# A causal mask of a chunked scan: one full mask product per group of heads against extra rows in the difference products plus 64x64 products on the diagonal

## The reference, cut to what matters

```
decay = exp(dt_t * a)
b_bar = dt_t[..., None] * b_t
state = decay * state + b_bar[..., None] * x_t[:, :, None, :]
y_t   = einsum('bhn,bhnp->bhp', c_t, state)
```

## Time and profile before

| | |
|---|---|
| median of 3 runs | 1465.38 us (1464.57 to 1468.33) |
| the profiled execution | 1465.41 us |
| its span, first to last instruction | 1463.4 us |
| TensorE matmuls, busy | 1403.8 us (8803 instructions) |
| TensorE weight loads, busy | 862.6 us |
| DVE / ACT / POOL, busy | 996.6 / 689.1 / 308.5 us |
| granted TensorE clock, mean | 0.988 of full speed |

### The profile page before, as it was taken

One profiled execution on the slowest core, in us unless ns is written; L12 is line 12 of the kernel. 1 busy time (PEld: TensorE's weight loads), 2 busy tenths in 40 slices (PEclk: granted clock), 3 DMA queues, 4 the chain that ended last, 5 costly groups with the idle time before them and its releaser, 6 DMA issues.

```text
span 1463.4 us, 23472 instructions
## 1 busy us (share of the span) xinstructions
PE 1403.8 (96%) x8803; PEld 862.6 (59%) x8803; DVE 996.6 (68%) x2849; ACT 689.1 (47%) x1351; POOL 308.5 (21%) x386
## 2 busy tenths in 40 slices
PE   8999999999999999999999999999999997999984
PEld 4447645676457665576456764576655763567543
DVE  2426797477874787477974778747874779747682
ACT  4443543645455562635436454555626354462312
POOL 3004201341104301142013411043011420133110
PEclk9999999999999999999999999999999998999998
DMA  8000001020000100020010200001000200101010
GB/s 299 10 0 30 15 15 48 3 75 29 26 23 17 61 30 26 22 78 15 15 48 2 76 30 26 22 18 61 29 26 22 77 15 15 47 4 46 29 48 4
DMA packets 47552, 54.24 MB, mean 37 GB/s; under 512 B 7625, under 2 KB 42313, under 8 KB 47441
## 3 DMA queue, kind: packets, MB, share of 16 engines
q1 hardware_dynamic: 41424, 46.41, 9.5%
q0 software_dynamic: 6016, 6.35, 1.7%
HBM read 34.84 MB, written 17.85 MB: 36 GB/s over the span
## 4 chain that ended last, share of the span: by engine, by line
PE 85%; DVE 8%; issue 4%; ACT 1%; POOL 1%; DMA 0%; POOLq 0%; SPq 0%; DVEq 0%
PE ps L1563 41%; PE ps L1729 8%; PE ps L1678 5%; PE ps L1637 4%; PE ps L1630 4%; DVE yst L1166 3%; PE ps L1690 2%; PE ps L1649 2%; PE ps L1869 2%; PE ps L1879 2%; PE ps L1664 2%; PE ps L1655 2%; PE ps L1668 1%; PE ps L1834 1%; PE ps L1800 1%
## 5 line engine op out<-in xcount | busy, mean ns | idle before, releaser
L1563 PE MATMUL ps<-xT,wb_s 128*128 128x512 f32 x512 | 232.9, 601 | 3.6 <-ACT xT L722 3.5
L1563 PE MATMUL ps<-xT,wc_s 128*128 128x512 f32 x512 | 225.4, 593 | 0.0
L1563 PEld LDWEIGHTS ps<-xT,wc_s 128*128 128x128 f32 x512 | 96.1, 190 | 112.3 <-issue 111.9
L1563 PEld LDWEIGHTS ps<-xT,wb_s 128*128 128x128 f32 x512 | 94.1, 191 | 113.1 <-issue 104.5
L1047 DVE SCALAR_TENSOR_TENSOR xT<-xc,cols_s,xT 128x512 f32<-128x512 f32 x192 | 134.8, 748 | 2.7
L1563 PE MATMUL ps<-hT,wx_s 128*128 128x512 f32 x256 | 117.7, 603 | 1.6 <-ACT hT L680 1.2
L1563 PE MATMUL ps<-hT,wz_s 128*128 128x512 f32 x256 | 112.8, 593 | 0.1
L1729 PE MATMUL ps<-CT,xT 128*128 128x256 f32 x512 | 111.9, 379 | 0.9 <-DVE xT L1226 0.9
L747 ACT ACTIVATE BT<-ps 128x512 f32<-128x512 f32 x64 | 37.9, 592 | 150.4 <-PE ps L1563 150.4
L1729 PEld LDWEIGHTS ps<-CT,xT 128*128 128x128 f32 x512 | 97.2, 190 | 17.8 <-issue 5.0
L788 ACT ACTIVATE XB<-ps 128x512 f32<-128x512 f32 x64 | 38.3, 599 | 138.0 <-PE ps L1649 138.0
(11 more groups left out here) (299 smaller groups left out, 2637.5 us busy)
## 6 DMA issues: line engine op xcount, KB each, us to landing
xr<-x SPq DMA_DIRECT2D x8, 1024.0 KB, 9.2
x_scratch<-xr SPq DMA_DIRECT2D x32, 256.0 KB, 2.1
out<-EC SPq DMA_DIRECT2D x32, 256.0 KB, 2.1
BT<-x SPq DMA_DIRECT2D x7, 1024.0 KB, 5.6
modrow<-mod_scratch SPq DMA_DIRECT2D x8, 512.0 KB, 6.6
w_s<-w SPq DMA_DIRECT2D x2, 1024.0 KB, 11.5
BT<-x SPq DMA_DIRECT2D x2, 512.0 KB, 5.2
xT<-wmod SPq DMA_DIRECT2D x1, 1024.0 KB, 9.4
```

Source lines behind the costliest of these rows:

```text
L1563: ins = t_.matmul(bank[:, :], w[:, k, m * P:(m + 1) * P], rhs[:, k, half * HALF:(half + 1) * HALF], start=k == 0, stop=k == nk - 1)
```

## The change

The full mask products are gone. The mask of a 128x128 block (source token j on the partitions, target token i along the columns) has four 64x64 blocks: j < 64, i >= 64 is never masked; j >= 64, i < 64 is masked as a whole; the two on the diagonal are the same triangle. The wholly masked block now comes out of the difference products by one more row per head: `Lsrc` has 1 in its columns 24 to 27 (of each half) for tokens 64 to 127, `Rsrc` has -1e30 there for tokens 0 to 63. These rows were zeros and were part of the products already. The two triangles are added by 64x64 products with the identity, one for each bank and each diagonal block, with 4 x 64 columns that stand 128 apart in the bank. The difference products now open the banks, and the wait for `Eg_ready` stands ahead of them.

```diff
-SP_ALL = 46
+SP_ALL = 50
...
+            for half in range(2):
+
+                block = slice(64 * half + 2 * ROWS, 64 * half + 2 * ROWS + NG)
+                link(g.memset(Lsrc[64:128, :, block], 1.0))
+                link(g.memset(Rsrc[0:64, :, block], MASKED))
...
                     for s in range(2):
                         if c or later(b):
                             pe.wait_ge(Eg_ready, at(Eg_ready, b, 2 * (c - 1) + s + 1 if c else 0))
-                        t_.matmul(ps[s][:, :], identb[:, :], causal[:, :, :].rearrange("p a n -> p (a n)"),
+                        r = slice(64 * s, 64 * s + 64)
+                        t_.matmul(ps[s][:, :], Lw[r, c * P:(c + 1) * P], R8[r, :, c * P:(c + 1) * P],
                                   start=True, stop=False)
                     for s in range(2):
                         r = slice(64 * s, 64 * s + 64)
-                        t_.matmul(ps[s][:, :], Lw[r, c * P:(c + 1) * P], R8[r, :, c * P:(c + 1) * P],
-                                  start=False, stop=True).then_inc(cd_filled, 1)
+                        for d in (slice(0, 64), slice(64, 128)):
+                            ins = t_.matmul(ps[s][d, :].rearrange("p (a n) -> p a n", a=NG)[:, :, d],
+                                            identb[r, r], causal[r, :, r], start=False, stop=True)
+                        ins.then_inc(cd_filled, 1)
```

## The result

The changed kernel takes 1451.96 us (median of 5, 1450.73 to 1456.53) against 1465.38; the ratio is 0.9911, 95% interval 0.9892 to 0.9930. The forecast was 1452.7 us. The profiled execution took 1451.82 us, its span is 1450.0.

What follows compares the result with a forecast made beforehand. TensorE was taken to bound the scan. Gains of 9.4 us (56 chunks), 2.8 (first chunks of 7 scans) and 0.5 (first scan) sum to 12.7 us: 1465.4 to 1452.7 us, range 1445 to 1462.

Steps and rivals of the forecast that it cites:

- TensorE bounds the scan: Inside a scan every piece of the chain is TensorE, 5.59 us per chunk; shortening its stream shortens the kernel.
- Difference products behind the transposes: In cumdiff, 0.10 us for a change of shape that used to be free, plus 0.213 us for both products.
- Change of shape from 64x128 to 64x64: In cumdiff, between difference and block products: between 0 and 0.10 us, taken as 0.10.
- X: Time of the four block products in cumdiff: 0.06 us of staggered starts plus 0.107 us of columns, 0.17 us.
- The first chunk of each scan: At a scan's start ps[0] is ready 0.40 us earlier and ACT's chain moves along; 7 x 0.40 = 2.8 us.
- The first scan: Its first chunk's groups took about twice as long, the 1.2 GHz level; gain taken as 0.5 us.
- The setup costs nothing: Four POOL memsets, 0.9 us in all, lie under 4.0 us of cover in the setup, so nothing.
- DVE keeps its place: In the scan's later chunks DVE has 0.95 us to spare over two periods, 0.61 over one; it holds.
- Rival 5: DVE becomes the bound from a gain of 0.47 us per chunk on, which no case reaches; no chance stated.
- half the gain: Block products at half column speed or loads one by one, 0.27 us; gain 6.3 us, 1459.1 us; chance 14%.
- one after another, with loads hidden or open: Block products do not overlap: loads hidden 0.43 us, 1468.0 us, chance 5%; loads open 0.73 us, 1488 us, chance 7%.
- Rival 1: Free change from 64x128 to 64x64, four block products fully parallel; gain 22.9 us, 1442.5 us; chance 12%.

Runs made afterwards that it cites:

- double blocks: The changed kernel with its four block products issued twice, one group of four behind the other; 1459.4 us, 0.9947 of the kernel before.
- one row half: The changed kernel with all four block products on rows 0 to 63 of the array; 1459.1 us, 0.9934 of the kernel before.
- rows only: The kernel before with only the four memsets for the extra rows added, full mask products kept; 1466.1 us, ratio 0.9998.

## Why the prediction was right, point by point

- **TensorE bounds the scan.** Shown. A pass of 256 columns put in (double blocks, one row half) came out as 0.11 us per chunk, and 5.8 to 7.0 us in all by the batch periods (7.1 and 7.4 by the medians). 0.11 x 56 is 6.2.
- **Difference products behind the transposes: 0.32.** Shown, in the profile after.
- **Change of shape from 64x128 to 64x64: 0.10.** Shown, as 0.12: 0.23 for the first four blocks, 0.11 for the second. The other bound, 0, is out.
- **X = 0.17: mis-sized.** It is 0.11, and with the change of shape 0.23 where the sum had 0.27. I had taken the pace from the state products, (0.61 - 0.10) / 16; but 0.15 of those 0.61 are the open load, so the pace was 0.029, and the four start together anyway. `cumdiff` costs 0.55 and not 0.58, the gain is 0.197 per chunk, 11.0 us and not 9.4.
- **The first chunk of a scan: 0.40 through ACT.** Measured 0.41, 7 times. Where the second `cumdiff` was put into this wait, the wait was gone and the scan shorter.
- **The first scan: 0.5.** From its first scores to the transposes behind `cumdiff` 2.24 us against 2.72: 0.48.
- **The setup costs nothing.** Shown by rows only. The memsets took 0.12 us each, and the setup of the changed kernel ended 0.56 us later.
- **DVE keeps its place.** Shown at this gain, with 0.56 and 0.41 us left (forecast 0.6 and 0.45). Rival 5, that DVE becomes the bound, needed 0.47 per chunk by my count; with state ahead of the transposes TensorE's chunk is 0.49 shorter than before and it does.
- **Sum.** 11.0 + 2.9 + 0.5 = 14.4, and 14.5 is what the end of the last scan shows. The last batch's tail gave 1.1 back in the profiled execution, with a granted clock of 0.89 there instead of 0.91. So that 12.7 came so near to 13.4 is in part luck: one term is too small by 1.6, and the tail's loss, which the sum did not have and which is not the edit's, hides most of it. The interval of the result, about 2.8 us to either side, holds both 12.7 and 14.4; the terms are told apart by the chains alone. What sets the clock in the tail is open.
- **Rivals 1 to 4.** Free change of shape and half the gain are out by double blocks; one after another, with loads hidden or open, is out by the four blocks' 0.30 us. Rival 1 was right on the overlap and wrong on the change of shape.

## What to carry to other kernels

Where TensorE is the bound, count a group of small matmuls by its passes of columns with the parts of the array that can run at once, and add about one weight load wherever the shape of the array parts changes. Then sort the groups so that equal shapes stand side by side. Here that, with the work that it put into TensorE's wait for ACT, was worth as much again as the smaller mask: 1.60 us per batch after 1.80, of which `cumdiff` ahead of the transposes had brought 0.50 in the scan's first chunk, mostly by that wait. And look at the first step of each loop apart, since another engine's queue can set it, and work put into that wait can be nearly free: the scan's first chunk took 5.85 us with the second `cumdiff` in it and 6.35 with it behind, 0.50 less for products that cost 0.55.

## What the runs showed of the hardware that was not expected

- The gap at a change of shape goes with the first weight load behind it: 0.10 to 0.12 us ahead of bf16 weights (loads of 92 to 103 ns), 0.15 ahead of fp32 128x64 ones (138 ns), 0.20 ahead of fp32 128x128 ones (192 ns). The Trainium skill (TensorEngine Tiling (Array Packing), Key Properties) says that a change of mode drains the engine; these runs agree and give the size. The load behind a change begins 0.07 us before the last result in front, and without a change 0.27 us before it. That the load's length sets the gap's size is read from these three kinds of weights; no run here varied the load alone.
- Four 64x64 parts, split by rows and by columns at once and writing two banks, are fully parallel: 0.11 us for four times 256 columns.
- A load of 64 columns of bf16 takes 103 ns, no less than one of 128 (98 ns). The Trainium skill's rule that column tiling switches the fast weight load off (TensorEngine Tiling (Array Packing), Restrictions) fits that; the four loads of a group run together (0.11 us for x4).
